# A 5x5 depthwise convolution's K part in 64-row products, a new head and a reordered tail, in a two-layer attention kernel on one NeuronCore

## The reference

```python
# layer 1: linear attention over 2 x 16 heads of 8 channels
qkv = conv1x1(x, w_qkv)                                   # 384 channels: Q, K, V of 8 per head
agg = conv1x1(conv5x5(qkv, w_dw, groups=384, pad=2), w_pw, groups=48)
qkv = concat([qkv, agg], axis=1).reshape(B, -1, 24, H * W)
q, k, v = relu(qkv[:, :, :8]), relu(qkv[:, :, 8:16]), qkv[:, :, 16:]
v = pad(v, one more row of ones)
vk = einsum('bhdn,bhen->bhde', v, k)
out = einsum('bhde,bhen->bhdn', vk, q)
x = x + conv1x1((out[:, :, :-1] / (out[:, :, -1:] + 1e-15)).reshape(B, -1, H, W), w_proj)
# layer 2: softmax attention over the 256 pixels of an image
t, p = W_theta @ x + b_theta, W_phi @ x + b_phi            # 64 channels each
f = softmax(einsum('ndq,ndk->nqk', t, p) / sqrt(64), axis=-1)
x = x + W_fuse @ einsum('nqk,nck->ncq', f, x) + b_fuse
```

## Time and profile before

| | |
|---|---|
| Time, median of 3 runs | 71.43 us (70.3 to 72.14) |
| The profiled execution, its own time | 71.04 us |
| Its span, first to last instruction | 69.1 us |
| TensorE busy | 62.6 us, 90% |
| VectorE, ScalarE, GpSimd busy | 39.1, 23.3, 22.5 us |
| Last TensorE matmul ends | 66.69 us into the span |

### The profile page before, as it was taken

One profiled execution on the slowest core, in us unless ns is written; L12 is line 12 of the kernel. 1 busy time (PEld: TensorE's weight loads), 2 busy tenths in 40 slices (PEclk: granted clock), 3 DMA queues, 4 the chain that ended last, 5 costly groups with the idle time before them and its releaser, 6 DMA issues.

```text
span 69.1 us, 2531 instructions
## 1 busy us (share of the span) xinstructions
PE 62.6 (90%) x1113; PEld 43.7 (63%) x1113; DVE 39.1 (57%) x98; ACT 23.3 (34%) x53; POOL 22.5 (33%) x36
## 2 busy tenths in 40 slices
PE   3999975999999999999899999999899999949950
PEld 2759953697668756656554666567584667828740
DVE  4760365218474582855319559786646567956260
ACT  0850236030245107613504000641021159698400
POOL 4404999989799999200000000000000000000000
PEclk9999999999999999999999999999999999999999
DMA  0874123410225681148300000000000000000243
GB/s 0 240 171 122 25 38 64 136 24 0 65 58 110 173 214 34 28 93 230 118 0 0 9 0 9 0 0 9 0 0 0 0 0 0 0 0 0 76 140 88
DMA packets 4377, 3.93 MB, mean 57 GB/s; under 512 B 1744, under 2 KB 4064, under 8 KB 4368
## 3 DMA queue, kind: packets, MB, share of 16 engines
q1 hardware_dynamic: 3312, 2.98, 16.7%
q10 hardware_dynamic: 544, 0.52, 2.6%
q0 software_dynamic: 512, 0.29, 2.1%
HBM read 1.24 MB, written 0.52 MB: 26 GB/s over the span
## 4 chain that ended last, share of the span: by engine, by line
PE 83%; ACT 5%; DVE 5%; issue 2%; DVEq 0%; ACTq 0%
PE bank L730 9%; PE bank L750 9%; PE bank L772 9%; PE bank L762 6%; PE bank L1007 6%; PE bank L708 5%; PE bank L741 4%; PE bank L944 4%; PE bank L821 3%; PE bank L811 3%; PE bank L985 3%; PE bank L975 3%; PE bank L781 3%; PE bank L966 3%; PE bank L914 3%
## 5 line engine op out<-in xcount | busy, mean ns | idle before, releaser
L750 PE MATMUL bank<-planes,wconv 32*32 32x256 f32 x288 | 6.6, 397 | 0.7 <-ACT planes L446 0.7
L730 PEld LDWEIGHTS bank<-wqkv_t,xp 128*128 128x128 f32 x48 | 6.4, 211 | 1.2 <-issue 0.9
L730 PE MATMUL bank<-wqkv_t,xp 128*128 128x128 f32 x48 | 7.0, 300 | 0.0
L772 PE MATMUL bank<-planes,wpair 64*32 64x256 f32 x192 | 6.4, 393 | 0.0
L750 PEld LDWEIGHTS bank<-planes,wconv 32*32 32x32 f32 x288 | 4.0, 103 | 2.4 <-DVE wconv L579 1.0
L446 ACT ACTIVATE planes<-bank 128x512 f32<-128x512 f32 x6 | 3.7, 641 | 4.8 <-PE bank L741 3.7
L1007 PE MATMUL bank<-pt,gf 128*128 128x256 f32 (+1 forms) x20 | 4.3, 352 | 1.0 <-ACT pt L513 1.0
L708 PE MATMUL bank<-warm 128*128 128x256 f32 x8 | 4.0, 654 | 1.2 <-DVE warm L522 1.2
L440 ACT ACTIVATE toks<-bank 128x512 f32<-128x512 f32 x4 | 2.4, 597 | 7.3 <-PE bank L730 7.3
L772 PEld LDWEIGHTS bank<-planes,wpair 64*32 64x32 f32 x192 | 3.3, 105 | 2.3 <-issue 1.0
L944 PE MATMUL bank<-qs,m 128*128 128x256 f32 x16 | 4.6, 408 | 0.0
(11 more groups left out here) (113 smaller groups left out, 113.7 us busy)
## 6 DMA issues: line engine op xcount, KB each, us to landing
planes<-planes SPq DMA_DIRECT2D x8, 180.0 KB, 3.1
xs<-in_x ACTq DMA_DIRECT2D x2, 256.0 KB, 3.2
wpair<-wnext SPq DMA_DIRECT2D x8, 48.0 KB, 2.5
out<-ys SPq DMA_DIRECT2D x3, 128.0 KB, 1.7
wqkv_n<-in_L_conv_w_qkv SPq DMA_DIRECT2D x3, 64.0 KB, 2.6
consts<-in_shape_constants POOLq DMA_DIRECT2D x1, 184.0 KB
wproj_n<-in_L_conv_w_proj SPq DMA_DIRECT2D x1, 128.0 KB, 2.3
tap_all<-tap_base SPq DMA_DIRECT2D x8, 9.6 KB
```

What stands on the lines that cost most here:

```text
L730: last = nc.tensor.matmul(bank[:, TOK[kind][pair], a * P:(a + 1) * P], xp[:, pair, a, :], wqkv_t[:, kind, :], start=True, stop=True)
L750: last = nc.tensor.matmul(bank[32 * quad:32 * (quad + 1), i, 0:NPIX], wconv[rows, quad, n, :], window(rows, K, quad, n // WIN, n % WIN), s ...
L772: last = nc.tensor.matmul(bank[32 * quad:32 * (quad + 1), 2 * h + j, 0:NPIX], wpair[rows, kind, j, quad, u, :], window(rows, plane_set(kin ...
```

## The change

The three windows of K's column v = 2 stay 32-row products (`convolve_last_column(K)`), the columns v = 0 and v = 1 become 64-row products (`convolve_pairs(K)`), as for Q and V. K gets a second plane, four twin copies (SyncE) and four weight copies (GpSimd), and its weights are made by two multiplications on VectorE and two on GpSimd instead of one on VectorE. `k_relu` is made by ScalarE from the banks, no longer by GpSimd from `planes`. In the head both `by_pixel(K)` stand ahead of the taps, the fourth zero matmul is 64 columns instead of 256, with a transpose of the identity behind it, and the border memsets stand behind the pixel copies. TensorE's middle, the end of layer 1 and layer 2 have a new order, and one of the two `values` copies goes from ScalarE to VectorE. Cut to its core, with round brackets where lines are put in words:

```diff
@@ setup @@
+SHORT = 64
...
-        wconv = sb("wconv", P, QUADS, WIN * WIN, 4 * E)
...
-        planes = sb("planes", P, 2 * KINDS - 1, PLEN)
+        planes = sb("planes", P, 2 * KINDS, PLEN)
...
-        PLANE = {K: (2, 3), Q: (6, 7), V: (6, 7)}
+        PLANE = {K: (6, 7), Q: (6, 7), V: (6, 7)}
...
-        VK = ((5, 7), (2, 3))
+        VK = ((4, 7), (2, 3))
@@ SyncE, behind the first eight shifted_taps copies @@
+            sp.wait_ge(border_zero, 3)
+            sp.wait_ge(plane_dve[K], 2)
+            twins(K, 1)
+            sp.wait_ge(plane_act[K], 2)
+            sp.wait_ge(column_mm, 1)
+            twins(K, 0)
             sp.dma_start(wfuse_n[:, :], w_fuse).then_inc(ld_wl1, 16)
...
+            sp.dma_start(consts[:, N_VALID:N_CONST], const_in[:, N_VALID:N_CONST]).then_inc(ld_const, 16)
             for kind in (Q, V):
...
+            (the five bias loads bth, bph, bfu)
@@ GpSimd @@
-            (the load of consts and the five bias loads)
             pool.wait_ge(wpw_out, 1)
+            pool.wait_ge(wsel_out[K], 1)
+            for j in range(2):
+                nc.gpsimd.tensor_tensor(*column_weights(K, 0, wpair[:, K, j]), ALU.mult).then_inc(wconv_pool[K], 1)
+            pool.wait_ge(wconv_pool[K], 2)
+            pool.wait_ge(wconv_dve, 2)
+            for i in range(QUADS):
+                pool.dma_start(*pair_copy(K, i)).then_inc(pair_moved[K], 16)
             pool.wait_ge(wsel_out[Q], 1)
             kind_weights(Q)
...
-            nc.gpsimd.tensor_scalar_max(k_relu[:, :, :]..., inner, 0.0).then_inc(k_relu_out, 1)
@@ ScalarE @@
             plane(K, 1)
+            for half in range(2):
+                act.wait_ge(plane_dve[K], half + 1)
+                nc.scalar.activation(k_relu[:, 8 * half:8 * half + 8, :]..., bank[:, PLANE[K][half], :], ACT.Relu).then_inc(k_relu_out, 1)
             tokens(Q, 0)
+            tokens(V, 0)
             plane(Q, 0)
             plane(Q, 1)
             conv_first_rounds(K, 1)
-            tokens(V, 0)
+            plane(V, 0)
+            plane(V, 1)
...
-            act.wait_ge(natq_mm, 1)
+            act.wait_ge(natq_mm, 2)
             for bb in range(2):
-                (parity(rq[1], 1, 1 - bb) from natq_bank(0))
+                (parity(rq[1], 0, 1 - bb) from natq_bank(1))
...
-            for step, n in ((thetas, 0), (thetas, 1), (exponentials, 0), (values, 0), (exponentials, 1), (values, 1),
-                            (exponentials, 2), (transposed, 0), (exponentials, 3), (transposed, 1), (transposed, 2),
+            for step, n in ((thetas, 0), (thetas, 1), (exponentials, 0), (exponentials, 1), (exponentials, 2),
+                            (values, 0), (transposed, 0), (transposed, 1), (exponentials, 3), (transposed, 2),
                             (transposed, 3)):
@@ VectorE @@
-            (the three memsets of planes' borders, ahead of pixels(0))
...
             pixels(1)
-            kept_taps(K)
+            (the three memsets of planes' borders, six planes instead of five)
             dve.wait_ge(wpw_mm, 1)
             nc.vector.tensor_copy(wpw_t[:, :, :]..., bank[:, WPW_T, 0:GROUPS * E]).then_inc(wpw_out, 1)
+            kept_taps(K)
...
-            nc.vector.tensor_tensor(*conv_weights_k(), ALU.mult).then_inc(wconv_dve, 1)
+            nc.vector.tensor_tensor(*column_weights(K, 2, wlast[:, K]), ALU.mult).then_inc(wconv_dve, 1)
+            nc.vector.tensor_tensor(*column_weights(K, 1, wnext[:, K]), ALU.mult).then_inc(wconv_dve, 1)
+            dve.wait_ge(border_zero, 3)
+            plane_keys()      # for each half: wait plane_act[K], copy the bank into the second K plane, plane_dve[K] + 1
...
             kept_taps(V)
+            tokens(V, 1)
...
             plane(Q)
             conv_last_rounds(K, 1)
-            tokens(V, 1)
+            plane(V)
             (memsets of vk, sum of k_relu)
-            plane(V)
...
             guard(0)
+            (natq_mm 1: the two rq[1] halves from natq_bank(0))
             reciprocals(0)
-            (natq_mm 2: the two rq[1] halves from natq_bank(1))
...
-            for b in range(B):
+            for b in range(B - 1):
                 scale_q(b)
             (attend_sums(1, ...) four times, now a pair of images at a time)
+            scale_q(B - 1)
...
-            for step, n in (... (first_layer, 2), (phis, 0), (first_layer, 3), (maxima, 0), (phis, 1), (maxima, 1),
-                            (normalize, 0), (maxima, 2), (normalize, 1), (maxima, 3), (normalize, 2), (normalize, 3), ...
+            for step, n in (... (first_layer, 2), (first_layer, 3), (phis, 0), (phis, 1), (maxima, 0), (maxima, 1),
+                            (maxima, 2), (normalize, 0), (normalize, 1), (normalize, 2), (maxima, 3), (values, 1),
+                            (normalize, 3), ...
@@ TensorE @@
             weights(0)
-            keep_warm(1)
+            keep_warm(1, SHORT)
+            nc.tensor.transpose(bank[:, WARM, 0:P], ident[:, :], ident[:, :])
             by_pixel(K, 0)
-            (waits, key_taps())
             by_pixel(K, 1)
             (transpose of wpw_r)
+            (waits, key_taps())
+            pe.wait_ge(wpw_out, 1)
             to_planes(K)
             weights(1)
             weights(2)
             pe.wait_ge(wconv_dve, 1)
             pe.wait_ge(plane_act[K], 2)
-            convolve_keys(range(0, 3))
-            pe.wait_ge(wpw_out, 1)
+            convolve_last_column(K)
             pe.wait_ge(wt_out, KINDS)
+            pe.wait_ge(plane_dve[K], 2)
+            pe.wait_ge(k_relu_out, 2)
             by_pixel(Q, 0)
             by_pixel(Q, 1)
-            convolve_keys(range(3, 6))
-            to_planes(Q)
-            convolve_keys(range(6, 9))
             by_pixel(V, 0)
             by_pixel(V, 1)
+            to_planes(Q)
+            pe.wait_ge(pair_moved[K], 16 * QUADS)
+            pe.wait_ge(twin_moved[K], 16 * QUADS)
+            pe.wait_ge(wconv_pool[K], 2)
+            convolve_pairs(K, range(0, 3))
+            (plane_act[Q], plane_dve[Q])
+            to_planes(V)
             (wconv_pool[Q], conv_act, conv_dve)
             convolve_last_column(Q)
...
             plain_queries(0)
-            to_planes(V)
+            (wproj_out, wl1_out)
+            plain_queries(1)
             (pair_moved[Q], twin_moved[Q])
             convolve_pairs(Q, range(0, 3))
-            plain_queries(1)
...
-            convolve_pairs(V, range(0, 1))
             value_keys(0, vt0, kt0, 0)
             value_keys(0, vt0, kt0, 1)
             denominators(1)
-            convolve_pairs(V, range(1, 2))
+            convolve_pairs(V, range(0, 2))
...
-            project(0, 0), project(1, 0); value_keys(1, ..., 0), (..., 1); project(2, 0), project(3, 0)
-            wait vk_out[1] 4; projected_sums(1, 0), (1, 1)
+            project(0, 0); wait vt1_out 1; value_keys(1, ..., 0); wait vt1_out 2; value_keys(1, ..., 1)
+            project(1, 0), project(2, 0); wait vk_out[1] 2; projected_sums(1, 0); wait vk_out[1] 4; projected_sums(1, 1)
...
             project(0, 1), project(1, 1)
+            project(3, 0)
             project(2, 1)
+            project(3, 1)
             thetas_phis(0)
-            project(3, 1)
+            thetas_phis(1)
             scores(0)
-            thetas_phis(1)
+            scores(1)
             values(0)
-            scores(1)
             values(1)
             transpose_probs(0)
             transpose_probs(1)
+            transpose_probs(2)
             attend(0)
-            transpose_probs(2)
             attend(1)
```

153 lines of the change are left out of this document (75 added, 78 removed).

## The result

| | before | after |
|---|---|---|
| median of the runs | 71.08 us | 67.62 us (67.49 to 68.92) |
| ratio | | 0.958, 95% interval 0.950 to 0.966 |
| profiled execution | 71.04 us, span 69.1 | 67.49 us, span 65.7 |

The change makes the kernel 4% faster, 67.62 us where 67.5 was forecast. The ratio is of the fast executions of both kernels (three of the four after, 67.49 to 67.72 us), so it is not the quotient of the two medians. The sum is nearly right, its terms are not: the tail brought 2.0 us instead of 1.1, and two waits that were costed at nothing took 1.2 us back. The page of the kernel after, its busy times, is to be read beside the earlier trace rows: TensorE is busy for 3.2 us less, and the end comes 3.4 us earlier.

What follows compares the result with a forecast made beforehand. TensorE's list of work plus its few waits was taken as the bound. Gains of 0.9 + 1.37 + 0.3 + 0.1 + 1.1 = 3.8 us gave 67.2 to 67.6, stated as 67.5 us, range 66.5 to 69.6.

Steps and rivals of the forecast that it cites:

- Head, -0.9: Up to the first K product: it comes at 10.65 instead of 11.59 us, 0.9 us won (0.4 to 1.1).
- The 0.3 of the short zero matmul: Ahead of by_pixel(K, 0): a 64-column zero matmul with a transpose ends near 5.0 instead of 5.31, 0.3 us won.
- K's convolution, -1.37: K's nine windows at 6.4 us become one column and three rounds of pairs at 5.04, 1.37 us won.
- The wait for K's copies, 0: Ahead of K's pairs: twins and weights land before TensorE asks at 17.75, cost 0, 0.25 us to spare at worst.
- Rival 1: K's twins or weights late, TensorE stands at 17.75 before the pairs: about 1 us, 68.5 us; chance 0.2.
- VectorE nearly critical: In the head, from 8.85 to 12.4 us: VectorE's copies must precede by_pixel(Q), asked for at 12.8; cover 0.3 us.
- rival 2: VectorE bounds the new head, by_pixel(Q) starts 0.5 to 1 us late: 68.3 us; chance 0.15.
- if they swap: In the head, `wnext` issued after GpSimd's K multiplication: 0.84 us more on VectorE, 0.5 on TensorE.
- Ahead of V's last column, -0.3: TensorE's wait of some 0.4 us there goes, as plain_queries(1) moved earlier covers Q's copy: 0.3 us won (0 to 0.5).
- the 0.1 of V's joined rounds: V's convolution: rounds 0 and 1 joined win 0.18 us at most, taken as 0.1.
- The tail, -1.1: Layer 1's end and layer 2: reordered projections and earlier attend(0) end at 65.5 instead of 66.69, 1.1 us won (0.4 to 1.4).
- rival 4: TensorE's clock rises late in the new head: each us at the low level costs 1 us more; chance 0.05.

Runs made afterwards that it cites:

- best2: Changed kernel with GpSimd's K multiplications waiting for `wnext`, ScalarE issuing K's weight copies, `kept_taps(V)` behind `plane(Q)`, constants' load behind Q's twins: 67.23 us, ratio 0.951.
- keys32: Changed kernel with K's columns v = 0 and v = 1 as 32-row products in one uncut run, no copies for K: 71.57 us, ratio 1.007.
- gate_late_c: Changed kernel with GpSimd's K multiplications waiting for `wlast` and `wnext`, `kept_taps(V)` behind `plane(Q)`, constants' load behind Q's second two twins: 67.97 us, ratio 0.958.

## Why the prediction was right, and where not

- **Head, -0.9: right.** 10.73 for the first K product (10.65 forecast), ScalarE's plane copies deciding, with taps and both by_pixel in the order worked out. The 0.3 of the short zero matmul is not confirmed: 0.19 by the start of by_pixel(K), nothing at the first K product once the clock's rise is matched. So the order of the stages gave the 0.86. That it is read off fairly is chance: the clock record begins at 6.42 us in the trace of before and at 6.28 in that of after. With the rise as it fell out in the other kernels, the same head puts the first K product between 10.25 and 11.23.
- **K's convolution, -1.37: right as a stage length.** The column is 2.13 in the chain at Q, pairs 2.99 at K (with the start of its first records) and 2.92 at Q, 22 and 30 ns a record. The floor on the Trainium skill's page "TensorE: Matmul & The Clock Gate", section "Wait — 56ns, not 53.3ns?", would have given 2.4 us; the rows held.
- **The wait for K's copies, 0: wrong, by 1.04 us.** Rival 1 came true at its price, though its releaser was the twins. The step that failed is "the last is issued at about 13.6" and "2.7 to 3.7 us to landing". TensorE asked at 17.79 (17.75 forecast), though by_pixel(Q) had waited, since the four by_pixel took 3.65 us instead of the 3.96 forecast. By the prediction's own numbers the last issue is at 13.75, not 13.6, as four issues of 0.6 from 11.95 outlast the wait for column_mm. The last twin went out at 14.6, not 13.6: VectorE's plane copies were 0.45 us late through `wnext`, and SyncE's issues took up to 0.95 instead of 0.6. It took 4.1 us to landing, where the slowest of before had 3.7 and K's own twins without the weights' copies beside them 3.2. The prediction named this case, "if both queues hold each other up", priced it at 1 us and gave it no place in the sum. A cover of 0.25 us at the worst of the rows was taken for safe, but the rows of before had less traffic beside them.
- **VectorE nearly critical: right as rival 2, undersized as a mechanism.** The wait was 0.17 us, since by_pixel(Q) had 0.3 of cover. The condition was put as "if they swap", a start behind GpSimd's. It is paid from 0.7 us ahead of that. Up to 1.58 us was paid in other kernels, three times the 0.5 named.
- **Ahead of V's last column, -0.3: right**, 5.51 us from Q's pairs to V's column became 4.18, of which 1.06 is plain_queries(1), moved ahead, and 0.27 the wait. The "some 0.4 us" that the prediction read there was too much: its row has 0.21 of idle time. V's column itself took 2.47 us in the chain instead of 2.13, a standstill as described under best2, which ate the 0.1 of V's joined rounds: 10.78 us from its start to spread(), before and after.
- **The tail, -1.1: right in the projections, half missing behind them.** project(b, 1) starts 4.65 us behind by_token(V), 5.82 before; the masks' products on VectorE start 1.23 behind value_keys(1), as forecast, and attend(0) starts 4.5 us ahead of the end (4.7 forecast). The step that failed is "the rest of TensorE's list up to values(1) ends at 59.0": it moved records without a price for the switches between them, 0.21 us each. Counted from by_token(V), that list ended at 12.7 us where 13.85 was forecast. The same prediction had taken 0.18 for joined V rounds, so the rows to see it by were at hand.
- **The clock, rival 4: did not occur** as a loss. The slow records are there, the last of 421 ns at 5.88 us in the kernel after, just short of the prediction's sign ("past 6 us"), but the kernel before had them as long (the last at 6.17). In other executions the moment lay between 4.0 and 7.3 us, worth 1.2 us of by_pixel(K). Behind 1.7 us of standstill the clock fell once more, in keys32.

The forecast of 67.5 was met so closely by luck: +0.9 of the tail and -1.2 of the waits nearly cancel. The range was wide enough for either miss alone (68.7 and 66.6).

## What to carry to other kernels

Count the switches between kinds of TensorE work as well as the work; in a reordering they can be nearly half of the gain (0.85 of 2.0 us here). When a gain moves a transfer onto the path, price its queue's issues and landing under the new traffic, with more than the slowest row of before. A wait moved away from one stage shows up at the next late thing: look which engine's list is the second bound before crediting it in full. And when two executions differ early in the span, look at the durations of equal records and not only at the clock row.

## What was not expected of the hardware

- The head differs between executions of kernels that are the same up to there. The 16 records of by_pixel(K) take 1.88 to 3.04 us, since 1 to 11 of the first of them last 304 to 583 ns instead of 275, up to the moment at which the clock record begins. In gate_late_c the trace has no clock record at all, and the durations alone show it. Their row (duration in ns, min/median/max), first in the kernel after, then in gate_late_c:

```profile
L753 PE MATMUL bank<-wqkv_t,xp x16: 274/275/583, 4.9 to 7.3; 128*128 128x128 f32 x16
```

```profile
L755 PE MATMUL bank<-wqkv_t,xp x16: 274/421/582, 4.7 to 7.7; 128*128 128x128 f32 x16
```

- A VectorE product of 24 elements lasted 2549 ns beside three GpSimd multiplications, 170 otherwise. One line of the kernel after:

```profile
L563 DVE TENSOR_TENSOR wsel<-tap_all,consts x12: 165/170/2549, 12.6 to 18.7; 128x24 f32<-128x24 f32 x12
```

- TensorE can stand still inside a stage, 0.2 to 2 us, with no semaphore to wait for, ahead of the same record in different kernels and 1.2 to 1.6 us behind the end of a transfer on the instruction queue. A stage that "waits for nothing" but takes longer than its twin is worth a look at the distances between starts.
- A DMA issue on SyncE takes 0.53 us or up to 1.87, on ScalarE up to 1.37, with the same transfers; SBUF copies of 180 KB land 2.6 to 4.8 us behind their issue.
